# A two-layer gated attention and expert kernel: the second layer's norms move from VectorE to ScalarE, and its rounds begin at half step 260

## The reference, cut to what matters

```python
def reference(x, ctx_2048, mask_full, mask_BxS2_bk0, g_xattn, g_ffn, ...):   # x is 32 x 64 x 256
    x = x + tanh(g_xattn[0]) * L0_xattn(layernorm(x), ctx_2048, ctx_2048, ...)
    x = x + tanh(g_ffn[0])   * L0_ffn(layernorm(x), router_w, gate_w, up_w, down_w)   # 8 experts, top-p
    x = x + tanh(g_xattn[1]) * L1_xattn(layernorm(x), ctx_2048, mask_BxS2_bk0)
    x = x + tanh(g_ffn[1])   * L1_ffn(layernorm(x), gate_up_proj, down_proj)          # 4 experts
    return x

def layernorm(x, eps=1e-05):
    return (x - mean(x)) / sqrt(var(x) + eps)
def L1_xattn(h, mem, mask):
    a = softmax(where(mask, h @ mem.T / 16, -1e30))
    return where(any(mask), a @ mem, 0)
def L1_ffn(x, gate_up, down):       # token n of a sequence goes to expert n % 4
    gate, up = split(x4 @ gate_up)
    return (silu(gate) * up) @ down
```

## Time and profile before

| what | us |
|---|---|
| median of three runs before | 853.85 |
| lowest and highest of them | 850.92, 854.37 |
| the profiled execution | 856.54 |
| its span in the trace | 854.8 |
| TensorE busy, of the span | 775.1 (91%) |
| VectorE busy | 687.9 (80%) |
| ScalarE busy | 596.3 (70%) |
| GpSimd busy | 580.0 (68%) |

### The profile page before, as it was taken

One profiled execution on the slowest core, in us unless ns is written; L12 is line 12 of the kernel. 1 busy time (PEld: TensorE's weight loads), 2 busy tenths in 40 slices (PEclk: granted clock), 3 DMA queues, 4 the chain that ended last, 5 costly groups with the idle time before them and its releaser, 6 DMA issues. The chain is left out here.

```text
span 854.8 us, 30113 instructions
## 1 busy us (share of the span) xinstructions
PE 775.1 (91%) x11511; PEld 722.5 (85%) x11511; DVE 687.9 (80%) x2385; ACT 596.3 (70%) x1298; POOL 580.0 (68%) x617
## 2 busy tenths in 40 slices
PE   3457689999999999999999999999999999888886
PEld 2335579999999999989999999999999999777875
DVE  4765778888888888888888888888888886898973
ACT  3376768778787878777787878787877773454442
POOL 4374638787979797969788888888888664222321
PEclk9555689999999999999999999999999999999999
DMA  7689998879899888888997978797888764110002
GB/s 235 184 181 245 238 214 187 142 142 159 147 157 151 152 161 145 152 142 160 152 170 131 173 137 177 126 173 147 149 146 166 121 110 128 51 63 14 26 5 96
DMA packets 319540, 122.99 MB, mean 144 GB/s; under 512 B 274716, under 2 KB 312612, under 8 KB 319396
## 3 DMA queue, kind: packets, MB, share of 16 engines
q1 hardware_dynamic: 318656, 120.53, 73.0%
q10 hardware_dynamic: 740, 0.54, 0.3%
HBM read 45.53 MB, written 8.39 MB: 63 GB/s over the span
## 5 line engine op out<-in xcount | busy, mean ns | idle before, releaser
L592 POOL TENSOR_TENSOR p_parts<-p,p_parts 128x512 f16<-128x512 f32 x256 | 296.6, 1158 | 111.2 <-ACT p_parts L707 99.2
L849 PE MATMUL psG<-xT,w_gu 128*128 128x128 f16 x3072 | 193.5, 220 | 7.4 <-DVE th_ga_h L1287 7.0
L584 POOL TENSOR_TENSOR hp_lo<-th_ga_h,hp_hi 128x512 f16<-128x512 f32 x136 | 157.6, 1159 | 57.3 <-ACT hp_hi L729 54.0
L849 PE MATMUL psU<-xT,w_gu 128*128 128x128 f16 x3072 | 193.4, 220 | 1.4 <-DVE th_ga_h L1295 1.3
L849 PEld LDWEIGHTS psG<-xT,w_gu 128*128 128x128 f16 x3072 | 176.4, 98 | 12.0 <-DVE th_ga_h L1287 9.9
L849 PE MATMUL psY<-w_dn,hp_hi 128*128 128x256 f16 x1024 | 181.7, 273 | 0.8 <-POOL hp_lo L584 0.8
L849 PEld LDWEIGHTS psU<-xT,w_gu 128*128 128x128 f16 x3072 | 176.7, 98 | 3.1 <-DVE th_ga_h L1295 2.6
L707 ACT ACTIVATE p_parts<-p 128x512 f16<-128x512 f32 x256 | 160.5, 627 | 6.5 <-DMA p_turn<-p_parts 5.7
L1211 DVE CUSTOM_DVE_ANT_0 ps<-ps,mask_in 128x256 f32<-128x256 f32 x256 | 104.2, 448 | 57.1 <-PE ps L849 56.6
L849 PE MATMUL psY<-w_dn,hp_lo 128*128 128x256 f16 x512 | 139.5, 273 | 0.0
L699 ACT ACTIVATE p<-psT,exp_bias 128x256 f32<-128x256 f32 x256 | 107.3, 472 | 41.1 <-DVE exp_bias L1215 33.4
(11 more groups left out here) (180 smaller groups left out, 1093.5 us busy)
## 6 DMA issues: line engine op xcount, KB each, us to landing
mask_in<-in_mask_Bx2048x_ff SPq DMA_DIRECT2D x32, 256.0 KB, 3.2
part_scratch<-parts SPq DMA_DIRECT2D x16, 384.0 KB, 4.0
q_stack<-part_scratch SPq DMA_DIRECT2D x62, 96.0 KB
k_stack<-part_scratch SPq DMA_DIRECT2D x62, 96.0 KB
stage<-in_L_ffn_gate_w SPq DMA_DIRECT2D x8, 512.0 KB, 4.9
stage<-in_L_ffn_up_w SPq DMA_DIRECT2D x8, 512.0 KB, 4.6
stage<-in_L_ffn_down_w SPq DMA_DIRECT2D x8, 512.0 KB, 4.8
p_turn<-p_parts SPq DMA_TRANSPOSE x256, 3.7
```

The source lines that it names most:

```text
L584: pool.tensor_tensor(hp_lo[:, u % 2, :], hb32[:, u % 2, :], hp_hi[:, u % 2, :], ALU.subtract).then_inc(s["h_split"], 1)
L592: pool.tensor_tensor(p_parts[:, g % 4, 1, :, :], p32[:, g % 2, :, :], p_parts[:, g % 4, 0, :, :], ALU.subtract).then_inc(s["plo_done"], 1)
L849: return pe.matmul(out_, lhsT, rhs, start=start, stop=stop, skip_group_check=shares_bank)
```

## The change

Four things change.

- `late_norm` moves from VectorE to ScalarE (an Identity activation with a scale and a bias for each row). For its bias VectorE writes the negated mean (`cnm`) ahead of `cve`, and GpSimd, behind the power and after waiting for its end, multiplies the two (`csh`). The wait `pow3_done` or `pow4_done` now stands for both.
- `late_masks` moves from r = -2 to r = 1.
- `late_base` is 261 for round 0 and 260 + 4t for the others, where it was 264 + 4t. So round 0 begins three half steps sooner and each other round four, and rounds 0 and 1 are three half steps apart, the others four. The late units, `Y_OUT_AT` and `Y_TURN_AT` are drawn in. The half steps of the weight cut stay.
- The loads of the masks and of the first two contexts are issued one step (eight half steps) sooner.

```diff
-LATE_SLOTS = [N_UNITS + at for at in (0, 1, 2, 3, 5, 6, 9, 10)]
-Y_OUT_AT = [8 * TAIL_STEP + at for at in (26, 33, 37, 44)]
-Y_TURN_AT = [8 * TAIL_STEP + at for at in (32, 36, 38, 45)]
+LATE_SLOTS = [N_UNITS + at for at in (0, 1, 2, 3, 4, 5, 7, 8)]
+Y_OUT_AT = [8 * TAIL_STEP + at for at in (26, 30, 34, 40)]
+Y_TURN_AT = [8 * TAIL_STEP + at for at in (28, 32, 35, 41)]
...
-            return 8 * TAIL_STEP + 4 * t
+            return 8 * TAIL_STEP + (4 * t - 4 if t else -3)
...
-                if n == TAIL_STEP - 2:
+                if n == TAIL_STEP - 3:
                     open_late()
                     for t in range(2):
                         load_late_ctx(t)
...
                 pool.wait_ge(s[f"ln{3 + kind}_in"], t + 1)
-                pool.tensor_tensor(crs[:, kind, :], cve[:, kind, :], minus_half[:, 0:2], ALU.pow
+                if t:
+                    pool.wait_ge(s[f"xn{3 + kind}_ready"], 2 * t)
+                st.link(pool.tensor_tensor(crs[:, kind, :], cve[:, kind, :], minus_half[:, 0:2], ALU.pow))
+                pool.tensor_tensor(csh[:, kind, :], cnm[:, kind, :], crs[:, kind, :], ALU.mult
                                    ).then_inc(s[f"pow{3 + kind}_done"], 1)
...
+            def late_norm(t, kind):
+                act.wait_ge(s[f"pow{3 + kind}_done"], t + 1)
+                if t:
+                    act.wait_ge(s[f"xn{3 + kind}T"], t)
+                for u in range(2):
+                    act.activation((xn3, xn4)[kind][:, u, :], x_res[:, 2 * t + u, :], ACT.Identity,
+                                   scale=crs[:, kind, u:u + 1], bias=csh[:, kind, u:u + 1]
+                                   ).then_inc(s[f"xn{3 + kind}_ready"], 1)
...
+                st.link(dve.tensor_scalar(cnm[:, kind, :], cmv[:, kind, :, 0], -1.0, None, ALU.mult))
                 dve.tensor_scalar(cve[:, kind, :], cmv[:, kind, :, 1], EPS, None, ALU.add).then_inc(s[f"ln{3 + kind}_in"], 1)
...
                         if r == -2:
                             late_stats(t, 0)
+                        elif r == 1:
                             late_masks(t)
-                        elif r == -1:
-                            late_norm(t, 0)
```

More of the change, by code:

```diff
@@ L222, in build @@
         cve = lb("cve", [P, 2, 2], F32)
+        cnm = lb("cnm", [P, 2, 2], F32)
+        csh = lb("csh", [P, 2, 2], F32)
         crs = lb("crs", [P, 2, 2], F32)
@@ L816, in step @@
                     for t, r in late_at(n, i):
-                        if r == 0:
+                        if r == -1:
+                            late_norm(t, 0)
+                        elif r == 5:
+                            late_norm(t, 1)
+                        elif r == 0:
                             late_copy("xn3T", t, x3T[:, :, :, :].rearrange("p u k t -> p (u k t)"), psT[:, :], "xt3_done")
@@ L1343, in late_stats @@
                     dve.wait_ge(s["y_used"], 2 * NE * (t + 1))
+                if t:
+                    dve.wait_ge(s[f"pow{3 + kind}_done"], t)
                 for u in range(2):
@@ L1463, in step @@
                             late_stats(t, 1)
-                        elif r == 5:
-                            late_norm(t, 1)
                         elif r == 7:
```

## The result

The changed kernel takes 856.87 us in the median of 13 runs (854.46 to 858.21); the kernel before, beside it, 853.83 (850.92 to 855.48). The ratio is 1.0029, with a 95% interval of 1.0018 to 1.0040: slower by 0.3%. One execution of the changed kernel in that set took 1538.79 us, and one of the kernel before, beside the last two experiments, 1294.46; no ratio counts them, and without the first the median of the second set is 855.98 and not 856.26. The forecast was 853.6, a hair under no change; the time lies inside the range of 848.5 to 859.0, but the interval excludes the forecast.

What follows compares the result with a forecast made beforehand. TensorE was taken to bound before the rounds, VectorE once rounds and weight cuts run together. Terms from 730.46 (+3.2, +7.4, -1.1, 12.95, tail +0.3) summed to 854.5 against 854.8, giving 853.6 us by the median; range 848.5 to 859.0.

Steps and rivals of the forecast that it cites:

- The wait before the low cut: In cut rounds, VectorE ready at 3.50 waits for ScalarE's high cut and begins the low cut at 5.97.
- the price of a round without a cut: From masked row to masked row 11.74 us, against 12.49 and 12.09 before; two rounds together -1.1 us.
- way to round 1's masked row (f = 3.2): Round 0's work in front delays round 1's masked row by 3.2 us, bounds 2.0 to 5.5.
- first round with a cut: The round behind the first cut becomes 2.7 us longer, with a late high cut and round 0's low part.
- round 7's masked row to the tail: From the last round's masked row to the gate product that opens the tail: 12.95 us, bounds 11.5 to 14.5.
- tail: From that gate product to the span's end: keeps its form, 18.28 us, plus 0.3 for a down product and turn.
- the rule on the price: ScalarE norms by the skill's formula cost 0.40 us, not 0.59; seven rounds about 2 us shorter; not adopted.
- rival of the port: VectorE and GpSimd hold each other where masks meet the kind 1 product: +2.9 us at most, 854 to 857.
- Priced at nothing: Earlier mask and context loads on the SP queue cost nothing; if cover is gone, one stall up to 2 us.
- The cut waits are hidden: Rival: low cut begins at 3.50, cut rounds 13.3 us, whole 844; at least half hidden 844 to 850, chance 0.22.
- Round 0 bare: Rival: ScalarE's queue in half step 263 exposes round 0's work, 858 to 862 us, chance 0.20.
- It doesn't do what it says: Rival that the change is not really carried out; excluded since the list shows the norms on ScalarE; no chance given.

Runs made afterwards that it cites:

- the second set: The changed kernel run again without an edit, beside the kernel before: 856.26 us, ratio 1.0025.
- the last two experiments: The runs e8 (844.66 us) and e9 (851.90 us), with the kernel before run beside them.
- The first experiment on it: The run e1_cut_first: ScalarE's high cut moved ahead of the rounds' work in the changed kernel, 848.13 us.
- e4_masks_back: The changed kernel with the masks back at r = -2, behind the first statistics: 855.59 us, ratio 1.0043.
- e1_cut_first: The changed kernel with the high part of the weight cut ahead of the rounds' work in ScalarE's list: 848.13 us, ratio 0.9930.
- e5_power_behind: e1_cut_first with GpSimd's power and product of norm kind 0 behind `hp_lo` instead of ahead of it: 845.49 us, ratio 0.9915.
- r1_again: The changed kernel run once more with no edit: 856.26 us, ratio 1.0025 to the kernel before.
- e6: e1_cut_first with the weight cuts two half steps sooner, in 265, 269, 273 and 277: 844.79 us, ratio 0.9903.
- e8: e6 with GpSimd's power and product of norm kind 1 one half step later, behind `hp_lo`: 844.66 us, ratio 0.9899.
- e9: e5_power_behind with the old schedule, rounds begun at half step 264 and loads as before: 851.90 us, ratio 0.9968.

## Why the prediction was wrong

The wait before the low cut was right in form and size, and the sum was still 1.8 us short, in a change whose sum was near nothing. So the sign was wrong: -0.3 forecast in the traced execution, +1.56 measured. Two steps failed. The first is the overlap of the moved masks: the prediction walked one cut round, in which VectorE stands idle before the masked row and hides them, and took that over to stretches where VectorE waits for nobody. There they count in full, 0.42 us on the way to round 1's masked row and 0.45 in the first cut round. The second is the price of a round without a cut, 11.74 us, where TensorE alone is busy 11.89 and the round takes 11.95. Together these are 1.3 of the 1.8 us; the rest is spread over the terms and stays open. Term by term:

| term | forecast us | measured us | miss |
|---|---|---|---|
| way to round 1's masked row (f = 3.2) | 28.80 | 29.43 | +0.63 |
| first round with a cut | 18.50 | 19.12 | +0.62 |
| three further rounds with a cut | 3 x 15.79 | 15.86, 15.88, 15.88 | +0.25 |
| two rounds without | 2 x 11.74 | 11.95, 11.96 | +0.43 |
| round 7's masked row to the tail | 12.95 | 12.81 | -0.14 |
| tail | 18.58 | 18.61 | +0.03 |

- **The wait before the low cut** was the main step, and it held: 2.35 us in place of the 2.47 that the two columns of that step imply (3.50 to 5.97), in three rounds. The power takes 0.70, where the walk had the 0.80 that it takes beside the masks. The first cut waits 3.86. Norms at 1.09 for two (the rows' price, and not the shorter one of the rule on the price), the product at 0.20, the masked row's wait of 1.86: all as walked. The first experiment on it took 8.1 us away.
- **f was mis-sized, by the masks.** Timeline of after, with the masked rows of rounds 0 and 1 and the first low cut:

```profile
720.04 0.30 DVE L1384 CUSTOM_DVE_ANT_0 psV<-psV,neg 128x128 f32<-128x128 f32 x1 [0.57 <-PE psV L867]
...
725.07 1.16 POOL L586 TENSOR_TENSOR hp_lo<-th_ga_h,hp_hi 128x512 f16<-128x512 f32 x1 [3.15 <-ACT hp_hi L734]
...
725.30 0.95 DVE L1393 TENSOR_TENSOR cr<-csum,valid 128x2 f32<-128x2 f32 x1
...
726.43 0.88 DVE L1397 SCALAR_TENSOR_TENSOR x_res<-psV,cr,x_res 128x256 f32<-128x256 f32 x2 [0.18 <-PE psV L867]
...
728.98 0.42 DVE L1375 SCALAR_TENSOR_TENSOR neg<-m_u,bd 128x256 f32<-128x256 uint8 x1
...
730.43 0.29 DVE L1384 CUSTOM_DVE_ANT_0 psV<-psV,neg 128x128 f32<-128x128 f32 x1
...
737.60 1.23 DVE L1355 SCALAR_TENSOR_TENSOR d_gu<-d_st,d_gu 128x1024 f16<-128x1024 f32 x1 [3.86 <-ACT d_dn L796]
...
746.98 0.42 DVE L1375 SCALAR_TENSOR_TENSOR neg<-m_u,bd 128x256 f32<-128x256 uint8 x1
```

  From 726.43 to the masked row at 730.43 VectorE waits for nobody, and the masks at 728.98 lie in between. The prediction named no masks here, and had VectorE's free time take nearly all that was added to it. In e4_masks_back, where they are written before round 0's masked row, the same way is 3.58 us in place of 4.00, and the whole way to round 1's masked row 0.41 shorter. That is two thirds of the 0.63; the rest stays open. The prediction's rival of the port shows here too, in a place where it was not looked for, and costs nothing: `cr`, 128 x 2, stands beside `hp_lo` and takes 0.95 in place of 0.16 (774.53 in a later round), but the instruction behind it still waits 0.18 for TensorE's `psV`. Where masks and products meet, the place that the rival named, the product takes its 0.20 (778.22).
- **The first cut round** was priced with its masks hidden, as in the others, since VectorE waits 1.8 us before their masked row. In this round it waits for nothing: VectorE's work is end to end from the late low cut to the masked row at 749.55 (no bracket on it), for the last routing is in it too. The masks at 746.98 count in full there, 0.45 of the 0.62: from the low cut to the masked row it is 11.95 us, and 11.50 in e4_masks_back, where they stand ahead of the cut. (They count there too: the router's logits, `lg`, begin 3.15 us behind the masked row in place of 2.69, and the high cut follows them.) The walk of one round was carried over to a round whose last wait is another.
- **Rounds without a cut**: the walk had the scores at 10.64 from the masked row and the next one at 11.74; measured 10.79 (807.96) and 11.95. TensorE is busy 11.89 of that. The forecast said that its products "begin to limit" but priced the copy on ScalarE, and did not add up TensorE's own busy time, which before was 11.90 in the first of its two rounds of this kind (10.45 in the second). With late units drawn in to both, that sum made 11.74 doubtful before the run.
- **Priced at nothing**: the loads. Half steps 248 to 256 run at the same pace in both traces: from the gate product at 680.36 to the one at 701.00 it is 20.64 us after, from 684.21 to 704.86 20.65 before. That was right.
- **The rivals.** "The cut waits are hidden" did not come, but e1_cut_first is that rival made true, and it came out at 848, not 844: part of the rest was kept by `hp_lo`, a price that the rival left out, and e5_power_behind, without that, is at 845.5. "Round 0 bare" did not come. "It doesn't do what it says" was rightly excluded.
- **The span.** The forecast tied itself to the span of one execution, and its own sum was made against 854.8. Had the whole spans been compared, it would have read as a gain of 2.3 us. Only the stretch behind a common instruction shows the loss.

Of the 2.5 to 3 us by the medians, 1.56 is shown in the traces. The interval of the second set reaches down to 0.9 us and that of the first to 1.5, so the two are not at odds; the rest stays open.

## What to carry to other kernels

When work is moved to an idle engine, ask what it will stand in front of in that engine's list: here the move freed 1.8 us of VectorE a round, and put a chain of four dependent instructions ahead of the one thing that VectorE needed next; three lines written further up, and a power written further down, turned +6.0 us into -3.1. For a sum of small terms of both signs, add up the busy time of every engine in each kind of round as a lower bound, and walk each kind of round by itself, the first one above all. And compare two traces from a common instruction behind which the programs differ, when the part ahead of it varies by more than the effect.

## What the runs showed of the hardware

**VectorE and GpSimd hold each other, mostly for whole instructions.** The low cut of `d_gu` (two inputs from SBUF, 1024 elements) takes 1.21 to 1.23 us clear of GpSimd's `hp_lo`, 1.90 when it begins 0.34 us into it, 2.21 when it begins 0.03 into it; both times it ends 1.08 us behind the end of `hp_lo`, so it did hardly anything until then. `cr`, begun 0.23 into it, ends 0.02 behind it, and `cnm` (0.47) 0.03. The other way round `csh` takes 0.87 and ends 0.05 behind the low cut that had begun first. The Trainium skill, page SBUF — State Buffer, section SBUF: two separate sides, has it so: the pair of ports is locked, by whichever of the two starts first, for the whole instruction, against VectorE instructions with two inputs from SBUF or in a two-port mode. The traces agree for these (that `cnm`, with one input, runs in such a mode is not shown), but not for the power, 128 x 2 on GpSimd: beside the masks in e4_masks_back, which had begun 0.17 us ahead of it and last 0.42, it takes only 0.10 longer (0.80 for 0.70), where the rule would have it wait 0.25; and begun 0.36 us ahead of a low cut (777.27 in e5_power_behind) it does not stretch that at all (1.23). Nor does it stretch the masks that begin 0.44 into it in after (0.42, at 777.89), and the product takes its 0.20 though it begins 0.09 before the end of those masks (778.22).

**TensorE's granted clock fell to half within a round, and it cost nothing.** In two of the changed kernel's cut rounds the window's clock is 0.89, where before it was 1.00; the one at 765.41 stands above. The next has the same length at full clock:

```profile
775.00:776.00 1.00, 1.00 (x11) 0.94 (x8) 0.97 (x3) 0.00 (x0) 0.00 (x0) 0.60 0.00 0
776.00:777.00 1.00, 1.00 (x6) 0.74 (x5) 0.86 (x5) 0.00 (x0) 0.00 (x0) 0.50 0.00 0
...
781.29:797.17 15.88, 12.19 (x148) 10.69 (x147) 11.14 (x35) 8.46 (x19) 4.01 (x6) 1.00 0.07 20
```

0.50 is the lower level, 1.2 GHz. Ahead of the fall TensorE had stood 2.05 us for `up_mul` (row 773.83 above) and had begun again at full clock (1.00 in 774:775). While it was low, two down products took 0.63 for 0.38 elsewhere, and four context turns 1.03 for 0.60; TensorE's busy time grew from 12.19 to 13.29 in the round, into time in which it would have waited for VectorE. What such a fall costs where TensorE is the limit, no run here shows. In r1_again it comes in the first and second cut rounds (0.91 and 0.89) where in after it came in the second and third, and the rounds are the same within 0.03 us. In the cut rounds of e1, e5, e6, e8 and e9 the clock stays at 1.00.
